# Non-local block: reassociating the value path, and a new order for all five queues

## The reference

```python
theta = einsum('bhwc,cd->bhwd', x, W_theta)              # 256 -> 32
phi   = maxpool2x2(einsum('bhwc,cd->bhwd', x, W_phi))    # 256 -> 32, 1024 -> 256 cells
g     = maxpool2x2(einsum('bhwc,cd->bhwd', x, W_g))      # 256 -> 128, 256 cells
beta  = softmax(einsum('bqd,bkd->bqk', theta, phi), axis=-1)   # 1024 queries, 256 cells
tmp   = einsum('bqk,bkv->bqv', beta, g)                  # 1024 x 128
o     = einsum('bhwv,vc->bhwc', tmp, W_o)                # 1024 x 256
return gamma * o + x
```

## Time and profile before

| what | us |
|---|---|
| median of 3 runs | 233.02 (231.57 to 233.1) |
| the profiled execution | 233.71 |
| its span, first to last instruction | 231.9 |
| busy: TensorE / VectorE / GpSimd / ScalarE | 223.1 / 184.7 / 168.0 / 137.8 |
| DMA, mean over the span | 246 GB/s |

### The profile page before, as it was taken

How to read it: one execution, slowest core, us unless ns; L and a number is a source line. 1 busy time by engine, 2 the same in 40 slices (tenths; PEclk the granted TensorE clock), 3 DMA queues, 4 the chain that set the end, 5 groups by cost and what they waited for, 6 DMA issues and landing times.

```text
span 231.9 us, 4348 instructions
## 1 busy us (share of the span) xinstructions
PE 223.1 (96%) x1400; PEld 181.7 (78%) x1400; DVE 184.7 (80%) x463; ACT 137.8 (59%) x264; POOL 168.0 (72%) x121
## 2 busy tenths in 40 slices
PE   7989889999999999999999999999999999999894
PEld 4455786977969698796959879696988969679794
DVE  5588677987979799797869979786987978899685
ACT  3496847548293765839366483937657393665550
POOL 1569799949689595969849596895959598543680
PEclk9999999999999999999999999999999999999999
DMA  7943848969497896959788595979859581917754
GB/s 198 395 187 75 293 148 259 343 206 343 141 315 255 272 339 172 362 176 312 227 314 305 178 356 166 317 225 316 296 175 356 188 310 44 287 75 260 239 230 181
DMA packets 19637, 57.03 MB, mean 246 GB/s; under 512 B 3424, under 2 KB 4640, under 8 KB 19616
## 3 DMA queue, kind: packets, MB, share of 16 engines
q1 hardware_dynamic: 19216, 56.57, 72.7%
q10 hardware_dynamic: 400, 0.20, 0.3%
HBM read 33.88 MB, written 16.78 MB: 218 GB/s over the span
## 4 chain that ended last, share of the span: by engine, by line
PE 88%; DMA 4%; DVE 3%; ACT 2%; issue 1%; POOL 0%; DVEq 0%; POOLq 0%
PE out L421 18%; PE proj L246 11%; PE proj L288 11%; PE proj L421 8%; PE shift L381 7%; PE score L326 6%; PE proj L297 5%; PE shift L421 5%; PE score L421 4%; DMA theta<-neg_lo 4%; PE score L353 3%; PE proj L258 3%; PE score L432 2%; DVE neg_parts L791 1%; PE shift L288 1%; PE score L336 1%
## 5 line engine op out<-in xcount | busy, mean ns | idle before, releaser
L678 POOL TENSOR_TENSOR e_lo<-e_sb,e_hi 128x512 fp32r<-128x512 f32 x64 | 80.9, 1284 | 41.5 <-ACT e_sb L597 41.5
L673 POOL TENSOR_TENSOR x_lo<-x_t,x_hi 128x1024 fp32r<-128x1024 f32 x30 | 71.9, 2401 | 2.2 <-ACT x_hi L525 2.2
L594 ACT ACTIVATE e_hi<-shift 128x512 fp32r<-128x512 f32 x60 | 36.2, 603 | 21.4 <-PE shift L381 19.6
L791 DVE TENSOR_REDUCE neg_parts<-score 128x2 f32<-128x512 f32 x64 | 43.5, 685 | 3.7 <-PE score L326 2.2
L421 PE MATMUL out<-G_hi,e_hi 128*128 128x258 f32 x132 | 37.5, 284 | 1.3 <-DVE G_lo L803 1.2
L421 PE MATMUL out<-G_lo,e_hi 128*128 128x258 f32 x132 | 37.5, 284 | 0.0
L421 PE MATMUL out<-G_hi,e_lo 128*128 128x258 f32 x132 | 37.3, 283 | 0.0
L597 ACT ACTIVATE e_sb<-shift 128x512 f32<-128x512 f32 x60 | 36.3, 604 | 0.0
L817 DVE SCALAR_TENSOR_TENSOR y_sb<-out,r_sum,x_n 128x256 f32<-128x256 f32 x66 | 31.9, 484 | 3.8
L525 ACT CAST x_hi<-x_t 128x1024 fp32r<-128x1024 f32 x31 | 32.6, 1056 | 0.0
L246 PE MATMUL proj<-x_t,w_sb 128*64 128x512 f32 x112 | 27.1, 605 | 0.0
(11 more groups left out here) (118 smaller groups left out, 489.0 us busy)
## 6 DMA issues: line engine op xcount, KB each, us to landing
x_t<-in_xt SPq DMA_DIRECT2D x32, 512.0 KB, 7.0
x_n<-in_xn SPq DMA_DIRECT2D x32, 512.0 KB, 5.8
out<-y_sb SPq DMA_DIRECT2D x31, 512.0 KB, 3.5
theta<-theta_hi SPq DMA_DIRECT2D x56, 64.0 KB, 5.1
theta<-theta_lo SPq DMA_DIRECT2D x28, 64.0 KB, 3.9
phi<-phi SPq DMA_DIRECT2D x14, 32.0 KB, 5.1
theta<-neg_hi ACTq DMA_DIRECT2D x16, 4.0 KB
theta<-neg_lo SPq DMA_DIRECT2D x16, 4.0 KB
```

Of the source, the lines that this page charges most:

```text
L594: nc.scalar.activation(e_hi[:, i % 2, n, :], shift_bank(i, n)[:, :], ACT.Exp)
L673: nc.gpsimd.tensor_tensor(x_lo[:, i % 2, h], x_t[:, i % 3, h], x_hi[:, i % 2, h].bitcast(f32), ALU.subtract).then_inc(x_lo_ready, 1)
L678: nc.gpsimd.tensor_tensor(e_lo[:, i % 2, n, :], e_sb[:, n, :], e_hi[:, i % 2, n, :].bitcast(f32), ALU.subtract).then_inc(e_lo_ready, 1)
L791: v.tensor_reduce(neg_parts[:, 2 * n:2 * n + 2], score[n % 2][:, :].rearrange("p (t k) -> p t k", t=2), AX.X, ALU.max, negate=True).then_i ...
```

## The change

The value path is associated to the left. The pooled g (`g_max`, channels on partitions) is transposed by TensorE (`turn_g`, two transposes into the bank `mixed`), split (`g_high` on ScalarE, `g_low` now on VectorE), and multiplied by the exponentials: `mix(i, h)` gives tmp for 512 queries with 6 matmuls of 512 columns. tmp is split (`tmp_high` on ScalarE, `tmp_low` on VectorE), and `outputs(i, p)` multiplies it by `gamma * W_o`, 6 matmuls of 256 columns for a pair of query tiles, both in one bank. The row sums no longer come out of the outputs: `sums` on ScalarE takes the exponential of each tile's scores minus its maximum, in place in the score bank, and adds along the row. The score bank is free for the next pair only then (`sum_ready`). One `reciprocals` serves an image. The high maxima's DMA goes from ScalarE's queue to SP's.

All five lists are new. In the main loop, images now lie three turns apart (`mix` and `outputs` of `s - 3`, the values of `s - 1`, theta and phi of `s`); theta and phi stand behind the last outputs of a turn, and the values of that image in the next turn. The first five turns and the last image have orders of their own.

```diff
             def max_into_stack(i):
+                sp.wait_ge(neg_hi_ready, i + 1)
+                sp.dma_start(max_row(i, 0), neg_hi[:, :].bitcast(f32)).then_inc(neg_in[i % 3], 16)
                 sp.wait_ge(neg_lo_ready, i + 1)
...
+            for s in range(6, 16):
+                load_t(s, 0)
+                load_t(s, 1)
+                load_n(s - 3, 1)
+                store(s - 4, 0)
+                store(s - 4, 1)
+                theta_hi_into_stack(s - 1)
+                phi_and_lo_into_stack(s - 1)
+                max_into_stack(s - 2)
+                load_n(s - 2, 0)
...
+            def turn_g(i):
+                pe.wait_ge(g_pooled, 2 * i + 2)
...
+                for k in range(KC):
+                    last = nc.tensor.transpose(mixed[:, DV * k:DV * (k + 1)], g_max[:, i % 2, P * k:P * (k + 1)], ident[:, :])
+                last.then_inc(g_turned, 1)
...
+                if i > 0 or n > 1:
+                    pe.wait_ge(sum_ready, 4 * i + n - 1)
...
+            def mix(i, h):
...
+                for k in range(KC):
+                    pe.wait_ge(e_ready, 4 * i + KC * h + k + 1)
+                    for n, g in enumerate((g_hi, g_lo)):
+                        nc.tensor.matmul(mixed_bank(i, h)[:, :], g[:, i % 2, k, :], e_hi[:, i % 2, KC * h + k, :],
+                                         start=(k == 0 and n == 0), stop=False)
+                for k in range(KC):
+                    pe.wait_ge(e_lo_ready, 4 * i + KC * h + k + 1)
+                    last = nc.tensor.matmul(mixed_bank(i, h)[:, :], g_hi[:, i % 2, k, :], e_lo[:, i % 2, KC * h + k, :],
+                                            start=False, stop=(k == KC - 1))
+                last.then_inc(mixed_ready, 1)
+
+            def outputs(i, p):
...
+                for k in range(2):
+                    h, w = divmod(2 * p + k, HT)
+                    cells = slice(P * w, P * (w + 1))
+                    for n, (m, o) in enumerate(((tmp_hi, wo_hi), (tmp_hi, wo_lo), (tmp_lo, wo_hi))):
+                        last = nc.tensor.matmul(out_bank(i, 2 * p)[:, C * k:C * (k + 1)], m[:, h, cells], o[:, :],
+                                                start=(k == 0 and n == 0), stop=(n == 2), skip_group_check=True)
                 last.then_inc(out_ready, 1)
...
+            for s in range(6, 16):
+                shifted(s - 3, 3)
+                scores(s - 2, 3)
+                values(s - 1, 0)
+                mix(s - 3, 0)
+                turn_max(s - 2)
+                values(s - 1, 1)
+                mix(s - 3, 1)
+                outputs(s - 3, 0)
+                outputs(s - 3, 1)
+                scores(s - 1, 0)
+                turn_g(s - 1)
+                outputs(s - 3, 2)
+                shifted(s - 2, 0)
+                scores(s - 1, 1)
+                shifted(s - 2, 1)
+                outputs(s - 3, 3)
+                theta_phi(s)
+                shifted(s - 2, 2)
+                scores(s - 1, 2)
...
+            def sums(i, n):
+                act.wait_ge(max_ready, 4 * i + n + 1)
+                if i >= 2 and n == 0:
+                    act.wait_ge(r_ready, i - 1)
+                for k in range(2):
+                    t = 2 * n + k
+                    last = nc.scalar.activation(score[n % 2][:, NK * k:NK * (k + 1)], score[n % 2][:, NK * k:NK * (k + 1)], ACT.Exp,
+                                                bias=neg_parts[:, t:t + 1], accum_out=e_sum[:, i % 2, t:t + 1])
+                last.then_inc(sum_ready, 1)
...
+            def tmp_high(i, h):
+                act.wait_ge(mixed_ready, 2 * i + h + 1)
+                if i > 0:
+                    act.wait_ge(out_ready, 4 * (i - 1) + 2 * h + 2)
+                nc.scalar.copy(tmp_hi[:, h, :], mixed_bank(i, h)[:, :]).then_inc(tmp_hi_ready, 1)
...
+            for s in range(6, 16):
+                exps(s - 3, 1)
+                sums(s - 2, 0)
+                sums(s - 2, 1)
+                theta_high(s - 1)
+                exps(s - 3, 2)
+                phi_high(s - 1)
+                exps(s - 3, 3)
+                tmp_high(s - 3, 0)
+                neg_high(s - 2)
+                x_high(s, 0)
+                sums(s - 2, 2)
+                tmp_high(s - 3, 1)
+                sums(s - 2, 3)
+                x_high(s, 1)
+                g_high(s - 1)
+                exps(s - 2, 0)
...
+            for s in range(6, 16):
+                x_low(s - 1, 0)
+                e_low(s - 3, 0)
+                e_low(s - 3, 1)
+                x_low(s - 1, 1)
+                e_low(s - 3, 2)
+                e_low(s - 3, 3)
...
+            def reciprocals(i):
+                dve.wait_ge(sum_ready, 4 * i + 4)
+                v.reciprocal(r_sum[:, i % 2, :], e_sum[:, i % 2, :]).then_inc(r_ready, 1)
...
+            for s in range(6, 16):
+                finish(s - 4, 7)
+                g_low(s - 2)
+                maxima(s - 2, 2)
+                phi_pool(s - 1)
+                maxima(s - 2, 3)
+                g_pool(s - 1, 0)
+                theta_low(s - 1)
+                tmp_low(s - 3, 0)
+                neg_low(s - 2)
+                phi_low(s - 1)
+                g_pool(s - 1, 1)
+                tmp_low(s - 3, 1)
+                finishes(s - 3, (0, 1, 2, 3, 4, 5))
+                reciprocals(s - 2)
+                maxima(s - 1, 0)
+                maxima(s - 1, 1)
+                finish(s - 3, 6)
```

More of the change, by code:

```diff
@@ L18 @@
 STACK = THETA + 2
-GW = C + 2
 TP = 2 * DK
@@ L90, in shift_bank, with mixed_bank @@
[L90 to L93, removed]
+            return shift[1] if i < 2 and h == 1 else value
+        def mixed_bank(i, h):
+            return score[1] if i == LAST and h == 1 else mixed
         w_in, wo_in, warm_ready = sem("w_in"), sem("wo_in"), sem("warm_ready")
@@ L200, in _ @@
+            load_n(1, 1)
             max_into_stack(0)
[L201 to L215, removed]
+            load_t(3, 1)
@@ L494, in _ @@
-            output(LAST - 2, 1)
+            turn_max(1)
+            scores(2, 0)
+            outputs(0, 0)
+            scores(2, 1)
+            outputs(0, 1)
+            mix(0, 1)
+            scores(2, 2)
+            scores(2, 3)
+            shifted(1, 0)
+            shifted(1, 1)
+            values(3, 0)
+            shifted(1, 2)
+            outputs(0, 2)
+            shifted(1, 3)
+            outputs(0, 3)
+            turn_max(2)
+            turn_g(2)
+            theta_phi(3)
@@ new lines, in _ @@
+            mix(1, 0)
+            values(3, 1)
+            shifted(2, 0)
+            shifted(2, 1)
+            outputs(1, 0)
+            outputs(1, 1)
+            mix(1, 1)
+            shifted(2, 2)
+            values(4, 0)
+            scores(3, 0)
+            outputs(1, 2)
+            outputs(1, 3)
+            turn_g(3)
+            scores(3, 1)
+            theta_phi(4)
+            scores(3, 2)
+            scores(3, 3)
+            shifted(2, 3)
+            mix(2, 0)
+            turn_max(3)
@@ new lines, in _ @@
+            values(4, 1)
+            mix(2, 1)
+            outputs(2, 0)
+            outputs(2, 1)
+            turn_g(4)
+            shifted(3, 0)
+            shifted(3, 1)
+            outputs(2, 2)
+            outputs(2, 3)
+            shifted(3, 2)
+            scores(4, 0)
+            scores(4, 1)
+            theta_phi(5)
+            scores(4, 2)
+            for s in range(6, 16):
[18 more added lines that the diff above has]
+                scores(s - 1, 2)
@@ L495, in _ @@
+            scores(LAST - 1, 3)
+            shifted(LAST - 2, 3)
+            values(LAST, 0)
             turn_max(LAST - 1)
+            mix(LAST - 2, 0)
+            values(LAST, 1)
             scores(LAST, 0)
-            outputs(LAST - 2, (2, 3))
-            scores(LAST, 1)
-            output(LAST - 2, 4)
             shifted(LAST - 1, 0)
             shifted(LAST - 1, 1)
-            output(LAST - 2, 5)
+            mix(LAST - 2, 1)
+            scores(LAST, 1)
+            shifted(LAST - 1, 2)
@@ L511, in _ @@
             shifted(LAST, 1)
+            outputs(LAST - 1, 1)
             shifted(LAST, 2)
[L513 to L514 removed]
+            outputs(LAST - 1, 2)
             shifted(LAST, 3)
[L516 to L517 removed]
+            outputs(LAST - 1, 3)
+            mix(LAST, 0)
+            mix(LAST, 1)
+            outputs(LAST, 0)
+            outputs(LAST, 1)
+            outputs(LAST, 2)
+            outputs(LAST, 3)
```

758 lines of the change are left out of this document (384 added, 374 removed).

## The result

The changed kernel takes 235.25 us (median of 4 runs, 233.26 to 236.19), the kernel before 232.74 beside it: a ratio of 1.0111 [1.0076, 1.0145]. I had forecast 226.6. The profiled execution took 236.19, the longest of the four; its span is 234.4, those of the others are 231.5 to 233.8.

The account below looks back on a forecast made before the run. The kernel before was taken as bound by TensorE's matmul columns, with ScalarE having room. Start 36.8, twelve turns of 12.9 (154.8) and drain 33.9 gave span 225.5; plus 1.8 less 0.7 made 226.6 us, range 217 to 238.

Parts of the forecast that it names:

- the loop: In a turn: shift 0, four exponentials, two pairs of row sums, score pair 3, TensorE's work to next shift 0; 12.9 us.
- S: Time of one 256-column row-sum exponential on ScalarE, with bias from a tile and accumulator output: taken as 0.47 us.
- 11.02 + 4S: Shortest turn in us that the loop allows, with four row sums in it: 12.9 at S = 0.47.
- TensorE's own turn: TensorE's work per image after the change: 12.62 us for 13.28 before, 0.66 less.
- The sum: Whole kernel: start 36.8 us, 12 turns of 12.9 (154.8), drain 33.9; span 225.5, time 226.6.
- values and scores come earlier: In the start: reason given for theta and phi of image 3 at 36.8 us against 37.34.
- the 39 us: In the start: theta of image 3 later than this would show the prediction wrong, as the start had no row.
- The walk: In the start: the new order stepped through with the predicted durations, giving theta and phi of image 3 at 36.8 us.
- the serial part: In the drain: the last image's steps from row sums to store run serially, making 33.9 us against 32.42.
- Cheap row sums: Rival on ScalarE: S up to 0.40, so TensorE's 12.62 plus small waits sets the turn; 223 us; chance 0.20.
- the bound of the turn: Rival: eight row sums make ScalarE the bound, slower, 236 us at S = 0.60, 243 at 0.66; chance 0.21.
- late on SP: Rival: the maxima's transfer lands late, shift 0 waits 0.5 us each turn; 233 us, no change; chance 0.14.

Follow-up runs that it names:

- e4: Changed kernel with score pair 3 moved behind the first half of the values in the main loop's TensorE list: 234.47 us, ratio 1.0047.
- e6: Changed kernel with the row sums of all 16 images left out, one small exponential in each pair's place: 231.65 us (one run).
- e1: Changed kernel with 18 warm-up matmuls for 8: 234.22 us, ratio 1.0053.
- e11: Changed kernel with seven thrown-away 512-column matmuls in TensorE's waits in the drain: 234.72 us, ratio 1.0075.
- e8: Changed kernel with 16 warm-up matmuls, score pair 3 behind the first value half, and another order in the drain: 232.25 us, ratio 0.9989.
- e9: e8 with the drain's remaining TensorE waits filled by reordering and two low halves moved to VectorE: 231.25 us, ratio 0.9925.
- e5: Changed kernel with the row sums of the last two images left out, one small exponential in each pair's place: 234.85 us (one run).

## Why the prediction was wrong

- **The turn failed, at the price of the loop.** The loop itself was right: e4 moves score pair 3 out of its way, e6 takes out the row sums, and either way most turns are 12.9. S was right too, 0.45 for the 0.47 taken. But "11.02 + 4S" makes 12.82 at this S, and the turn shown takes 13.20 (13.24 on average over the nine), as the last accumulator read is not overlapped and the matmuls behind score pair 3 have small gaps. TensorE's own turn was priced too low as well: with the loop out of the way it is 12.99 (e4) or 12.94 (e6) on average and not 12.62, so against the 13.48 of the nine turns before TensorE saves about 0.5 us an image and not 0.66. That the stretch from image 3 to 15 took 155.94 for 154.8 is luck. The sum put twelve whole turns behind theta of image 3, and the stretch is 2.5 us short of that: 12 x 13.2 - 2.5 = 155.9.
- **The start failed, at "values and scores come earlier".** The first scores come 2.45 us later than before, the first shift at 25.69 and not near 22.5, and theta of image 3 at 41.36, past the 39 us that the prediction itself named as a sign of being wrong. The walk names neither the 3.02 us of waiting for the second half of x, which theta and phi of image 0, now one block, need, nor the slow clock behind it. e1 takes 2.3 us of it back and has theta of image 6 at 75.87, against 75.5 by the forecast. The rest of the miss at image 3 is about the 2.5 us of matmuls that now stand ahead of it; whether the walk had them in, the record does not show. The time from the first scores to image 3 is the same with no row sums (e6), so ScalarE is not its cause.
- **The drain failed, at the serial part.** The 25.7 us of work were about right: TensorE's list behind theta of image 15 comes to 26.0 at the prediction's prices. But the last matmul ends 32.50 us after theta of image 15, where it was 29.34 with 27.2 us of work at the same prices. The slow clock is 1.25 of that (e11), waits are 2.74 (1.25 before), and the rest is small pauses that the profile counts as busy, for TensorE shows 28.1 us busy there at full clock too (e8, e9). The tail behind the last matmul is 1.5 longer than before. The row sums are 0.7 of the drain (e5). Reordering won little: e9 still takes 35.36, 2.9 us more than before, and which waits must go for the rest stays open.
- **The rivals.** None came true, and all took the start and the drain from the same walk. Cheap row sums were to give 223 us; without any row sums the kernel takes 231.65. ScalarE did not become the bound of the turn: e4 leaves it its work and the turn is 12.9. The maxima were not late on SP: in the twelve turns TensorE waits for no transfer of theirs. That 235.25 lies in the range at all is luck, as the range reached that far only for ScalarE as the bound.
- **Sign and size.** The forecast gain was 6.4 us, and three misses of about 3 each turned it into a loss. Against the kernel before, the drain loses 4.7 us where the nine turns gain 2.1; the start is even and would have gained 2.3 without the slow clock (e1).

## What to carry to other kernels

Where a change shortens a steady turn and also rewrites how the pipeline fills and drains, the ends need their own rows: take their length from the kernel before as the first estimate, and ask of each instruction moved there what it now waits for. Cut stages where both orders have the same work behind them: a cut at image 3 made the turns look as forecast when they were not. At both ends of this kernel a wait of TensorE cost twice, once as idle time and once in the slower matmuls behind it, so matmuls whose result is thrown away can pay at the ends. And take the suspected cost away altogether (e6) before tuning around it: it showed in one run that the row sums, which all the rivals were about, were not where the ends lost their time.

## What the hardware showed

- A row sum on ScalarE appears as two instructions, 456 ns and 216 ns on average, that overlap so that one costs 0.45 us for 256 columns.
- Eight warm-up matmuls in 3.78 us and then 3.02 us of idle time left TensorE at half speed for the next 5 us (8.09 to 13.2); with eighteen in 7.06 us and no gap the same matmuls ran at full speed from their first. The Trainium skill (TensorE: Matmul & The Clock Gate, "Why this matters for your kernels") advises to keep TensorE from gaps; the trace agrees at both ends.
- In the drain, waits of 0.3 to 0.95 us between 203 and 211 us were followed by a clock of 0.58 from 212 to 215; with seven more matmuls in these waits (e11) it stayed at full speed. In the turns, where TensorE is busy for 13.16 of 13.19 us, the clock stayed at 1.00.
